# Layer 2 of a four-layer token mixer: value products moved directly behind the scores, a bank of their own for the values' projections, and output folds two a slot

## The reference, cut to what matters

```
q = z @ wq @ fcq_w + fcq_b          # 16 heads of 64
k = z @ wk @ fck_w + fck_b
v = z @ wv @ fcv_w + fcv_b
scores = einsum('bihd,bjhd->bhij', q, k) / sqrt(64)
attn = softmax(scores)
out = einsum('bhij,bjhd->bihd', attn, v)
return out.reshape(b, n, 1024) @ fco_w + fco_b
```

## Time and profile before

| | |
|---|---|
| median of 3 runs | 2967.23 us (2957.83 to 2970.3) |
| profiled execution | 2955.89 us, its span 2954.1 us |
| PE busy | 2644.4 us (90% of the span) |
| DVE busy | 1904.6 us (64%) |
| ACT busy | 1334.0 us (45%) |
| layer 2's slots | 1330 us to about 2137 us of the span |

### The profile page before, as it was taken

The page is one execution under the profiler, slowest core; times in us unless marked ns, Lnnn a source line. Parts: engine busy times, 40 slices in busy tenths (PEclk is TensorE's granted clock), DMA queues, the critical chain, the costliest instruction groups (busy, mean ns, idle before and its releaser), DMA issues.

```text
span 2954.1 us, 40833 instructions
## 1 busy us (share of the span) xinstructions
PE 2644.4 (90%) x14522; PEld 1730.0 (59%) x14522; DVE 1904.6 (64%) x3790; ACT 1334.0 (45%) x3445; POOL 1240.5 (42%) x1116
## 2 busy tenths in 40 slices
PE   6787799999999999978889999999988988988988
PEld 3475355555555555544446666665547876776766
DVE  5768477787786877648667777776555263646633
ACT  4565424434434434334446666664442223454433
POOL 2552367777777677626533333320001430323331
PEclk8898899999999999979999999999986876889888
DMA  4462200000000000047112222220002211212113
GB/s 163 154 196 89 96 1 1 1 1 1 1 1 1 1 1 1 1 151 160 38 44 66 71 66 70 66 62 29 1 33 98 82 57 30 60 32 62 33 46 95
DMA packets 172521, 159.34 MB, mean 54 GB/s; under 512 B 98736, under 2 KB 149296, under 8 KB 171504
## 3 DMA queue, kind: packets, MB, share of 16 engines
q1 hardware_dynamic: 149536, 90.70, 11.1%
q0 software_dynamic: 22784, 66.05, 7.2%
HBM read 126.94 MB, written 59.51 MB: 63 GB/s over the span
## 4 chain that ended last, share of the span: by engine, by line
PE 42%; DVE 7%; ACT 3%; issue 2%; another core or an unknown queue 1%; SPq 1%; DMA 0%; POOL 0%; DVEq 0%; ACTq 0%
PE bank L65 37%; PE bank L2094 4%; DVE work L2050 1%; DVE work L3330 1%; ACT L3272 1%; DVE weights_even L3330 0%; DVE work L2027 0%; ACT weights_odd L2978 0%; PE bank L2925 0%; DVE weights_odd L3380 0%; DVE work L3378 0%; SPq L3121 0%; DVE weights_odd L3378 0%; DVE work L3529 0%
## 5 line engine op out<-in xcount | busy, mean ns | idle before, releaser
L1533 POOL TENSOR_TENSOR work<-work 128x512 f32<-128x512 f32 x384 | 495.3, 1290 | 301.4 <-DVE work L1525 281.0
L65 PE MATMUL bank<-work 64*128 64x256 f32 (+5 forms) x4384 | 588.1, 351 | 24.0 <-DVE work L3529 7.2
L65 PE MATMUL bank<-weights_odd,normed_channels 128*128 128x512 f32 (+3 forms) x1152 | 516.2, 557 | 53.6 <-DVE work L1525 52.4
L65 PEld LDWEIGHTS bank<-work 64*128 64x128 f32 (+4 forms) x4384 | 411.6, 170 | 224.9 <-issue 141.0
L1525 DVE TENSOR_TENSOR work<-bank,work 128x512 f32<-128x512 f32 x360 | 244.5, 686 | 99.6 <-PE bank L65 95.7
L2064 ACT ACTIVATE work<-bank,work 128x256 f32<-128x256 f32 x512 | 236.0, 472 | 153.3 <-DVE work L2050 145.5
L65 PEld LDWEIGHTS bank<-weights_odd,normed_channels 128*128 128x128 f32 x1152 | 184.4, 195 | 182.8 <-DVE work L1525 95.3
L2050 DVE TENSOR_REDUCE work<-bank 128x2 f32<-128x512 f32 x256 | 165.4, 686 | 167.7 <-PE bank L65 149.2
L595 POOL DMA_INDIRECT weights_even<-in_L_Wx,expert_slots x112 | 113.1, 1010 | 337.0 <-PE bank L668 269.1
L1600 ACT ACTIVATE work<-bank,work 128x256 f32<-128x256 f32 x256 | 119.0, 470 | 286.2 <-DVE work L1587 286.0
L65 PE MATMUL bank<-weights_even,work 128*128 128x128 f32 (+5 forms) x1632 | 230.1, 301 | 19.8 <-ACT work L3078 7.0
(11 more groups left out here) (344 smaller groups left out, 4616.3 us busy)
## 6 DMA issues: line engine op xcount, KB each, us to landing
filter_matrices<-in_L_filters SPq DMA_DIRECT2D x24, 512.0 KB, 8.6
work<-filter_matrices SPq DMA_DIRECT2D x16, 768.0 KB
weights_even<-noted_rows SPq DMA_DIRECT2D x56, 132.0 KB
noted_rows<-in_empty SPq DMA_DIRECT2D x11, 660.0 KB, 10.5
noted_rows_in<-in_empty SPq DMA_DIRECT2D x8, 660.0 KB, 10.7
weights_odd<-noted_rows_in SPq DMA_DIRECT2D x40, 132.0 KB
work<-token_rows SPq DMA_DIRECT2D x16, 256.0 KB, 3.2
token_rows_out<-in_zeros SPq DMA_DIRECT2D x6, 640.0 KB, 20.5
```

The source lines that it names most:

```text
L65: return pe.matmul(out, lhsT, rhs, start=first, stop=last, skip_group_check=True)
L1533: gp.tensor_tensor(self.sum_of(p), self.sum_of(p), self.product_of(p), ALU.add).then_inc(s["l1_add"], 1)
```

## The change

It moves `tensor_times_v` one slot later (n+4) and puts it directly behind the scores, ahead of everything else in the slot. The values' projections get the bank `b_fo`, and qk keeps `b_misc`. The second half of a group's values is projected in rest 8 to 11 in place of 4 to 7. The outputs of all eight pairs of a group are kept in eight buffers in the other weights' region, and the folds run in the next group's slots with rest 4 to 7, two a slot (`tensor_folds`), in `b_fo`, whose use by values and folds takes turns. The loop has two more slots at its end.

```diff
+L2_FOLDS = (4, 8)
+L2_OUTPUTS = (2048, 2048 + L2_PAIRS * GW)
...
-        self.p, self.pt, self.o, self.mixed = work.ring(6), work.ring(4), region.ring(2), work.ring(GROUPS)
+        self.p, self.pt, self.mixed = work.ring(6), work.ring(4), work.ring(GROUPS)
+        self.o = Arena(k.regions[1], L2_OUTPUTS[1], L2_OUTPUTS[0]).ring(L2_PAIRS)
...
         g, rest = divmod(slot, L2_UNITS)
-        if 4 <= rest < 8 and 0 <= g < GROUPS:
-            yield "v", g, rest
+        if 8 <= rest < 12 and 0 <= g < GROUPS:
+            yield "v", g, rest - 4
         if 12 <= rest and g + 1 < GROUPS:
             yield "v", g + 1, rest - 12
...
-        return (self.b_misc, self.b_fo)[self.shared_count(slot, kind) % 2 if slot < 0 else 0]
+        return (self.b_misc, self.b_fo)[self.shared_count(slot, kind) % 2 if slot < 0 else kind == "v"]
...
         on.wait_ge(s["l2_pv"], 2 * pair + 2)
-        on.wait_ge(s["l2_fold"], pair - 1)
-        a.activation(self.o[pair % 2], self.b_o[:, :], ACT.Copy).then_inc(s["l2_o"], 1)
-
-    def tensor_fold(self, pe, on, pair):
-        s = self.k.sem
-        g, m = divmod(pair, L2_PAIRS)
-        on.wait_ge(s["l2_o"], pair + 1)
-        if m == 0:
-            on.wait_ge(s["l2_mixed"], g)
-        mm(pe, self.b_fo[:, :], self.Fo[:, m, :], self.o[pair % 2], first=m == 0, last=m == L2_PAIRS - 1).then_inc(s["l2_fold"], 1)
+        on.wait_ge(s["l2_fold"], pair - L2_PAIRS + 1)
+        a.activation(self.o[pair % L2_PAIRS], self.b_o[:, :], ACT.Copy).then_inc(s["l2_o"], 1)
+
+    def tensor_folds(self, pe, on, slot):
+
+        s = self.k.sem
+        g, at = slot // L2_UNITS - 1, slot % L2_UNITS - L2_FOLDS[0]
+        of_slot = L2_PAIRS // (L2_FOLDS[1] - L2_FOLDS[0])
+        if not (0 <= g < GROUPS and 0 <= at < L2_FOLDS[1] - L2_FOLDS[0]):
+            return
+        for m in range(of_slot * at, of_slot * (at + 1)):
+            on.wait_ge(s["l2_o"], L2_PAIRS * g + m + 1)
+            if m == 0:
+                on.wait_ge(*self.shared_free[1])
+                self.shared_free[1] = (s["l2_mixed"], g + 1)
+            mm(pe, self.b_fo[:, :], self.Fo[:, m, :], self.o[m], first=m == 0, last=m == L2_PAIRS - 1).then_inc(s["l2_fold"], 1)
...
-    FIRST, LAST = -6, L2_UNITS * GROUPS + 6
+    FIRST, LAST = -6, L2_UNITS * GROUPS + L2_FOLDS[1]
...
                 self.tensor_score(pe, on, n, 0)
                 self.tensor_score(pe, on, n, 1)
+            if (n := self.due(slot, 4)) is not None:
+                self.tensor_times_v(pe, on, n)
             self.tensor_shared(pe, on, slot, ("v",))
+            self.tensor_folds(pe, on, slot)
             if (n := self.due(slot, 2)) is not None:
                 self.tensor_turn(pe, on, n, 0)
-            if (n := self.due(slot, 3)) is not None:
-                self.tensor_times_v(pe, on, n)
             self.tensor_shared(pe, on, slot, ("qk",))
             if (n := self.due(slot, 2)) is not None:
                 self.tensor_turn(pe, on, n, 1)
-            if (n := self.pair_end(slot, 4)) is not None:
-                self.tensor_fold(pe, on, n)
             self.tensor_experts(pe, on, slot)
...
-            if (n := self.pair_end(slot, 3)) is not None:
+            if (n := self.pair_end(slot, 4)) is not None:
                 self.scalar_outputs(a, on, n)
-            if (n := self.pair_end(slot, 4)) is not None and n % L2_PAIRS == L2_PAIRS - 1:
-                self.scalar_mixed(a, on, n // L2_PAIRS)
+            if (g := event(slot, L2_UNITS + L2_FOLDS[1] - 1, L2_UNITS, 0, GROUPS)) is not None:
+                self.scalar_mixed(a, on, g)
```

## The result

| | before | after |
|---|---|---|
| median of 20 runs each | 2967.05 us (2944.03 to 2978.06) | 2979.57 us (2963.02 to 2987.67) |
| ratio, 95% interval | | 1.0048 [1.0031, 1.0064] |
| span of the profiled execution | 2954.1 us | 2981.4 us |

The change makes the kernel 12.5 us slower, as forecast (2979, +12). The page's first part shows nothing of it: TensorE (PE) is busy 2648.8 us where it was busy 2644.4.

What follows compares the result with a forecast made beforehand. PE was taken to bound slots 32 to 103, DVE and GpSimd to pace the early slots. Terms 6.8 + 2.1 + 3.1 + 0.8 + 0.1 - 1 gave +12 us on a 2967.2 us median: 2979, range 2956 to 2995.

Steps and rivals of the forecast that it cites:

- Prices and links: PE stage times and DVE copy delays: second turn starts at 4.67 us with values, 3.61 without values or folds.
- Slots 32 to 103: Steady slots of layer 2: second turn waits for the first turn's copy, +6.8 us over 4.5 groups.
- The direct change from row to column tiles at the price of any other: Behind the scores and value products: this tiling change costs no more than others; free or double would shift 0.1 a slot.
- Rival 2: New waits cost more, early slots +8 us, double-priced direct tiling change +10: 2990 to 2998 us; chance 0.15.
- Rival 1: The saved tiling change, 0.19 us a slot, reaches the end: 14 to 15 us faster, 2952 us; chance 0.15.
- Slots 104 to 127 and the keys: Slots 104 to 127 +2.1 us, keys' bias waits in five odd slots +3.1, later second turns in slots 126 and 127 +0.8.
- The six folds: Credit of 5.2 us for six folds gone from slots 117 to 127, set against the folds at the end.
- The early slots at -1: Slots before 32: moved folds and DVE's shifting waits together give -1 us, between -8 and +8.
- The end: Last value products start as before; eight folds in a row cost 5.3 us, less 5.2 credited: +0.1.

Runs made afterwards that it cites:

- e3_between: Changed kernel with values' projection and folds moved between the two turns, and DVE's copy ahead of the values' bias; ratio to before 0.9972.
- e6_two_banks: Changed kernel with the second turn of slots with rest 0 to 3 sent to the folds' bank; ratio to before 1.0064.
- e7_old_place: e4_one_fold with the value products put back between the turns and their outputs a slot earlier; ratio to before 1.0065.
- e4_one_fold: e3_between with one fold a slot in eight slots of a group instead of two in four; ratio to before 0.9924.
- e10_six_less: Kernel before without six folds of the first group, in odd slots 5 to 15; slots 0 to 31 took 166.3 us, one run.
- after_again: Changed kernel, unchanged, run on another chip beside the kernel before; median 2920.08 us, ratio 1.0066.
- e2_banks: Changed kernel with its order undone, value products between the turns again; values' bank and two folds a slot stay; ratio to before 1.0050.
- e8_last_folds: e4_one_fold with the last group's folds taken one a slot from slot 124 on; ratio to before 0.9938.
- before_again: Kernel before, unchanged, profiled on another chip, the one that ran the changed kernel again; median 2900.6 us.

## Why the prediction was right, and where its sum was not

By its steps, on the profile it was made from:

- *Prices and links.* The new row of scores and value products, the bias's wait, the copy and the second turn are within 0.02 us of what was worked out, in the slots with values (4.69 for 4.67). Slots with two folds last 7.05 and 6.83 for 6.18 and 6.82 with a projection and one fold, slots with neither 5.29 and 5.07 for 5.28 and 5.92. **Slots 32 to 103: +6.6, forecast +6.8.** Shown from the other side by e3_between and e6_two_banks: take what puts the copy off away, or the bank, and the time is won.
- *The direct change from row to column tiles at the price of any other.* Right: 2.09 from the scores to the projection, 2.08 forecast. Rival 2's double price is refuted.
- *Rival 1, the saving reaches the end.* Refuted for this kernel and confirmed as a mechanism: 0.20 us a slot (e7_old_place against e4_one_fold) once other work covers the copy.
- *Slots 104 to 127 and the keys.* +2.1, +3.1 and about half of the +0.8 make 5.6; measured +5.3 on the first chip, which looks right by luck: slot 113 ran at a granted clock of 0.68 before and 0.80 after. With both at the full clock it is +6.8. Of the 1.2 between, some 0.9 (an estimate, one fold) is the fold that stood in slot 127 before and now stands ahead of it. The keys' waits have the forecast size: slots 105 and 107 last 5.77 for 5.03 and 5.02, and slot 106's scores start 0.63 later than the turn ahead of them needs (1986.97 - 1985.88 - 0.46). They come in seven slots for five (113 and 117 too).
- *The six folds.* **The step that failed:** "In exchange six folds (5.2) are gone from slots 117 to 127". They are gone from the early slots: from slot 104 to 127 the change leaves twelve projections and eight folds where there were eight and twelve. e10_six_less shows what six folds are worth in the early slots without the waits for "remote": 2.8 us at the same clock, 4.4 as measured.
- *The early slots at -1.* Taken with the 5.2 the sum held -6.2 that the early slots should have had; they gave +0.2 on the first chip and -1.5 on the other, 0.0 with slot 11 at the same clock. What was left out is the second group, +4.5 on the other chip: PE was the bound there too, and none of its slots has the experts' products, so the waits for keys come there as well (0.67 ahead of a slot's scores at 1475.30 in after_again). On the first chip the first group wins 3.6 and the second loses 3.8; what the waits for "remote" hide of either no run here tells.
- *The end.* "the last value products start at about 2134.55 as before" was wrong. The folds' 5.3 were right (5.1 in e2_banks), but the value products come a slot later by the order, and that costs 2.2 here; in the slots from 128 on stand two turns with 0.88 between them and value products that wait 1.17 or 1.18 for the copy of the outputs. **+7.4, forecast +0.1** with the misplaced credit.

By the profile the layer costs +19.6 (+19.2 on the other chip), not +12. The first comparison of medians gives +12.5 with an interval from 9 to 19, the second +19.5 with one from 12 to 26. That the first median met the forecast to 1 us is luck: the mechanism and its price in slots 32 to 103 are right, the sum is too low by 7 to 8: about 2 at the end and 6.4 in the early slots on the first chip; about 2 at the end, 4.7 in the early slots and 1.2 in slots 104 to 126 on the other. The range held in either case.

## What to carry to other kernels

Where two steps on one engine wait for a copy of another between them, look at what stands ahead of the first and what between them: in this kernel the same product costs its full time ahead, and nothing between as long as it fits into the wait (in e8_last_folds a fold alone between the turns cost nothing, one beside a projection 0.6 to 0.7). Count the moved instructions slot by slot before crediting any, in all stretches and at both ends. Compare a stretch only when its granted clock is the same in both profiles. An order that saves time on the busiest engine is worth its price only when the wait it uncovers gets other work; here the projection and the folds moved behind the first turn, DVE's copy moved ahead of the bias, and one fold a slot turned a loss of 0.5 to 0.7% into a gain of 0.8%.

## What the hardware showed unexpectedly

The same kernel took 2967 us on one chip and about 2900 on the others, and 33 us of that lie in slots 0 to 31 of layer 2, where DVE waited for "remote" on the first chip alone (12 waits before the maxima, 18.2 us in all); slots 32 to 103 are the same to 0.1 us. That the waits are the cause of the 33 us is my reading; no run changes the loads. Another 9 to 27 us lie in layer 3 (814.3 against 787.7 to 805.1), where also runs on the later chips differ by 17 us; their cause wasn't looked for.

The clock falls in the same kernel in one profile and not in the next. In slot 11 of before_again PE ran for part of the slot at the lower of its two levels (1.2 for 2.4 GHz; eight value products 1.98 us busy for 1.08), after it had waited 2.29 us in slot 10. In before it had waited 1.96 us there and in e10_six_less 3.13, and the clock of slot 11 stayed at 1.00 in both.
